# Last six layers of a two-layer transformer kernel: the score band written into PSUM by ScalarE, value products joined per tile, and new orders

## The reference, cut to what matters

```python
def local_attention(q, k, v):          # per batch and head, n = 512 rows, w = 32
    bq = q.reshape(b, h, nw, w, d)
    bk2, bv2 = (look(bk), look(bv))    # window i sees windows i - 1 and i: 64 keys
    mask = (it < jb) | (it > jb + w) | (jb == -1)
    sim = jnp.einsum('bhwie,bhwje->bhwij', bq, bk2) * QK_SCALE
    sim = jnp.where(mask, -jnp.finfo(sim.dtype).max, sim)
    attn = jax.nn.softmax(sim, -1)
    out = jnp.einsum('bhwij,bhwje->bhwie', attn, bv2)

def attn_layer(x, Wqkv, qs, ksc, Wo):  # q and k: l2norm, scale, rotary
    ...
    return out @ Wo

def ffn_layer(x, g, bln, W1, b1, W2, b2):
    xn = (x - mu) / jnp.sqrt(var + 1e-05) * g + bln
    a, gate = jnp.split(xn @ W1 + b1, 2, -1)
    return a * jax.nn.gelu(gate, approximate=False) @ W2 + b2

for i in range(6):
    x = attn_layer(shift_tokens(x), Wqkv[i], q_scale[i], k_scale[i], Wo[i]) + x
    x = ffn_layer(shift_tokens(x), ln_g[i], ln_b[i], W1[i], b1[i], W2[i], b2[i]) + x
```

## Time and profile before

| what | us |
|---|---|
| median of 3 runs (2396.79 to 2399.0) | 2398.37 |
| span of the profiled execution | 2396.9 |
| PE busy in the span | 2203.9 |
| DVE busy | 1780.6 |
| ACT busy | 1719.1 |
| POOL busy | 1230.9 |

### The profile page before, as it was taken

One profiled execution on the slowest core, in us unless ns is written; L12 is line 12 of the kernel. 1 busy time (PEld: TensorE's weight loads), 2 busy tenths in 40 slices (PEclk: granted clock), 3 DMA queues, 4 the chain that ended last, 5 costly groups with the idle time before them and its releaser, 6 DMA issues.

```text
span 2396.9 us, 82108 instructions
## 1 busy us (share of the span) xinstructions
PE 2203.9 (92%) x33332; PEld 1567.5 (65%) x33332; DVE 1780.6 (74%) x3567; ACT 1719.1 (72%) x3982; POOL 1230.9 (51%) x2002
## 2 busy tenths in 40 slices
PE   6799679999976799999999999999999999999996
PEld 3487368888855566666766666666666666666662
DVE  3577377777777788888888888878888888888851
ACT  2255378888854678878888787777778888778771
POOL 0177010000001677776777776767777777767650
PEclk9899789999987899999999999999999999999997
DMA  2000021221102111112111121112111211122110
GB/s 88 10 1 1 22 98 53 80 80 53 71 2 82 30 51 51 51 47 58 51 53 42 54 72 48 45 44 60 50 41 39 75 53 51 36 64 60 40 33 22
DMA packets 40966, 117.73 MB, mean 49 GB/s; under 512 B 7952, under 2 KB 13392, under 8 KB 37776
## 3 DMA queue, kind: packets, MB, share of 16 engines
q1 hardware_dynamic: 40592, 112.49, 15.5%
HBM read 50.48 MB, written 2.23 MB: 22 GB/s over the span
## 4 chain that ended last, share of the span: by engine, by line
PE 49%; ACT 10%; issue 4%; POOL 2%; DVE 2%; DMA 1%; SPq 0%; ACTq 0%; POOLq 0%; DVEq 0%
PE w_psP L1785 12%; PE w_psT L1794 7%; PE w_psF L1729 6%; PE w_psO L1841 6%; PE w_psS L1812 5%; PE w_psF L1751 5%; PE w_psT L1823 3%; ACT w_pb L1893 3%; PE w_psF L1755 2%; PE w_psS L1803 2%; ACT w_sq L1868 1%; ACT L1893 1%; ACT L1917 1%; DMA w_xsf<-H 1%; ACT w_oT L1906 1%
## 5 line engine op out<-in xcount | busy, mean ns | idle before, releaser
L2055 POOL TENSOR_TENSOR w_ab<-w_ab,w_nrm 128x512 f32<-128x512 f32 x384 | 392.9, 1045 | 8.4 <-POOL w_nrm L84 8.4
L1893 ACT ACTIVATE w_pb<-w_psS,w_mx 128x64 f32<-128x64 f32 x1536 | 350.2, 338 | 2.8 <-DVE w_mx L1962 1.9
L2047 POOL TENSOR_TENSOR w_ab<-w_ab,w_bb 128x512 f32<-128x512 f32 x192 | 245.3, 1278 | 172.8 <-DVE w_bb L1946 171.1
L1958 DVE TENSOR_REDUCE w_nrm<-w_sq 128x8 f32<-128x512 f32 x384 | 249.5, 665 | 107.5 <-ACT w_sq L1868 107.3
L1868 ACT ACTIVATE w_sq<-w_psP 128x512 f32<-128x512 f32 x384 | 237.4, 618 | 84.7 <-DVE w_nrm L1958 42.5
L1785 PE MATMUL w_psP<-w_hi,w_xh 128*128 128x512 f32 x576 | 274.6, 477 | 25.0 <-POOL w_xl L2037 8.5
L2071 POOL TENSOR_TENSOR w_pb<-w_pb,w_sm 128x512 f32<-128x512 f32 x192 | 200.3, 1043 | 185.0 <-DVE w_sm L1971 184.5
L1794 PE MATMUL w_psT<-tables_all,w_ab 128*128 128x128 f32 x1536 | 242.0, 280 | 8.7 <-POOL w_ab L2055 4.0
L1197 DVE TENSOR_TENSOR e_glo<-e_hh,e_ghi 128x512 fp32r<-128x512 f32 x256 | 169.3, 685 | 93.0 <-ACT e_ghi L1151 92.9
L1794 PEld LDWEIGHTS w_psT<-tables_all,w_ab 128*128 128x128 f32 x1536 | 174.2, 141 | 87.3 <-ACT w_qT L1881 23.9
L1785 PE MATMUL w_psP<-w_lo,w_xh 128*128 128x512 f32 x576 | 231.1, 401 | 0.0
(11 more groups left out here) (294 smaller groups left out, 5348.5 us busy)
## 6 DMA issues: line engine op xcount, KB each, us to landing
X<-tables_layer SPq DMA_DIRECT2D x48, 384.0 KB, 3.5
X<-w_v SPq DMA_DIRECT2D x48, 384.0 KB, 3.5
e_gb<-gate_rows SPq DMA_DIRECT2D x16, 1024.0 KB, 4.7
e_raw<-in_w_moe SPq DMA_DIRECT2D x32, 256.0 KB, 5.1
w_raw<-in_w_qkv SPq DMA_DIRECT2D x20, 384.0 KB, 4.8
X<-tables_layer SPq DMA_DIRECT2D x48, 128.0 KB, 3.6
w_o<-in_w_o SPq DMA_DIRECT2D x6, 512.0 KB, 4.6
w_xs<-H SPq DMA_DIRECT2D x24, 128.0 KB, 3.3
```

The costliest lines, as they stand in the source:

```text
L1893: last = act.activation(pb[k % 2][:, n, :], psS[:, j, KEYS * q:KEYS * (q + 1)], ACT.Exp, bias=mx[:, n:n + 1])
L1958: dve.tensor_reduce(nrm[k // 2][:, 0, 8 * (i % 8):8 * (i % 8) + 8], sq[:, i % 2, :].rearrange("p (h d) -> p h d", d=DH), AX_X, ALU.add).th ...
L2047: pool.tensor_tensor(a, a, bb[:, i % 2, :], ALU.add).then_inc(s["ad"], 1)
L2055: pool.tensor_tensor(a, a, nrm[k // 2][:, 1, 8 * (i % 8):8 * (i % 8) + 8].unsqueeze(2).to_broadcast([128, 8, DH]), ALU.mult).then_inc(s["n ...
```

## The change

Three things change in `windowed_layers`.

1. The band: PE writes it once, ahead of all rounds. From then on a new ACT unit "Bw k" copies it from `band_bf` into psS behind the exps of block k, and S(k+1) adds its products to that copy. S waits for `s["bw"]` instead of `s["e"]`; Bw waits for `s["e"]` of its own block.
2. Value products: Av k is now one unit per tile, 64 matmuls for its two blocks, even and odd, and Ot one output copy per tile of 1024 columns. pT gets a third buffer. `s["av"]` and `s["ot"]` count tiles instead of blocks.
3. The orders of all five engines are new. The constants `halves` and `guesses`, which nothing here reads, are gone with their memsets.

```diff
--- before.py
+++ after.py
@@ -1537,8 +1537,6 @@
     ab = c.sb("w_ab", [128, 2, 4, 512])
     bb = c.sb("w_bb", [128, 2, 512])
     nrm = [c.sb(f"w_nrm{j}", [128, 4, 64]) for j in range(2)]
-    halves = c.sb("w_halves", [128, 64])
-    guesses = c.sb("w_guesses", [128, 64])
     qT = [c.sb(f"w_qT{j}", [128, PAIRS, 128]) for j in range(2)]
     kT = c.sb("w_kT", [128, PAIRS, WIN + N])
 
@@ -1551,7 +1549,7 @@
     pb = [c.sb(f"w_pb{j}", [128, PAIRS, KEYS]) for j in range(2)]
     mx = c.sb("w_mx", [128, PAIRS])
     sm = [c.sb(f"w_sm{j}", [128, PAIRS]) for j in range(2)]
-    pT = [c.sb(f"w_pT{j}", [128, 4, 128]) for j in range(2)]
+    pT = [c.sb(f"w_pT{j}", [128, 4, 128]) for j in range(3)]
     oT = c.sb("w_oT", [128, PAIRS, N])
     xsf = c.sb("w_xsf", [D, N])
     yn = c.sb("w_yn", [128, TILES, D])
@@ -1565,7 +1563,7 @@
     scl = c.sb("w_scl", [128, 2, 4, DH])
     first = oT[:, 0:6, :].rearrange("p a b -> p (a b)")
 
-    names = ("wa", "wf", "wo", "tab", "scl", "z", "xst", "wd", "wh", "wl", "xh", "xl", "y", "xs", "p", "sq", "ab", "rs", "ad", "nm", "t", "te", "vx", "s", "mx", "e", "r", "pn",
+    names = ("wa", "wf", "wo", "tab", "scl", "z", "xst", "bw", "wd", "wh", "wl", "xh", "xl", "y", "xs", "p", "sq", "ab", "rs", "ad", "nm", "t", "te", "vx", "s", "mx", "e", "r", "pn",
              "pt", "pte", "av", "ot", "f", "xf", "xsf", "yn", "xn", "gg", "hh", "out")
     s = {k: c.sem("w_s_" + k) for k in names}
     s_ve = [c.sem(f"w_s_ve{j}") for j in range(2)]
@@ -1621,30 +1619,30 @@
     ORDER = {
         "pe": """
...
-            V1.1 P2.0 g1-- Av5.0- T0.0 P2.1 a1-- At7.0- Av6.0- T0.1 P2.2 g2-- T0.2 Av7.0-""",
...
+            T2.2- P0.2 At1.0- P0.3 tr-- T2.3- Av0.0- T3.0- S4.0-""",
...
         "sp": """
-            VE2.0-- xd0.0 VE3.0-- wd0.0- t1-- VE0.0- tl- VE1.0- xfd--""",
+            wd0.0------------ tl-------------- xd0.0----------- xfd-------------- t1--------------
+            VE0.0------------- VE1.0------------- VE2.0------------- VE3.0-------------""",
     }
 
@@ -1698,7 +1696,7 @@
                         sp.dma_start(x_back, x_dram).then_inc(s["xst"], 16)
                 elif kind == "VE":
                     wait(sp, s["vx"], r * UV + 2 * k + 2)
-                    wait(sp, s["av"], r * NBLK + 2 * (k - 2) + 1)
+                    wait(sp, s["av"], r * TILES + k - 1)
                     sp.dma_start(v_even[k % 2][WIN:128, :], v[k][0:128 - WIN, :]).then_inc(s_ve[k % 2], 16)
                     if k:
                         sp.dma_start(v_even[k % 2][0:WIN, :], v[k - 1][128 - WIN:128, :]).then_inc(s_ve[k % 2], 16)
@@ -1723,7 +1721,7 @@
                 half = int(f[2])
                 if half == 0:
                     pe.wait_ge(s["wo"], (layer + 1) * 16)
-                    pe.wait_ge(s["ot"], (r + 1) * NBLK)
+                    pe.wait_ge(s["ot"], (r + 1) * TILES)
                     wait(pe, s["out"], r)
                 for pair in range(4 * half, 4 * half + 4):
                     last = pe.matmul(psF[:, :], w_o[:, pair, :], oT[:, pair, :], start=(pair == 0),
@@ -1797,11 +1795,7 @@
                 elif kind == "S":
                     t, e = k // 2, k % 2
                     pe.wait_ge(s["te"], r * UR + 4 * t + 4)
-                    wait(pe, s["e"], r * UE + 2 * k)
-                    for h in range(2):
-                        rows = slice(64 * h, 64 * h + QB)
-                        pe.matmul(psS[:, h, 0:4 * KEYS], c.ident_bf[rows, :], c.band_bf[rows, min(k, 1), :], start=True,
-                                  stop=False, skip_group_check=True)
+                    wait(pe, s["bw"], r * NBLK + k)
                     for g in range(2):
                         for n in range(2):
                             at = QB * (e + 2 * n)
@@ -1824,28 +1818,30 @@
                                             pb[k % 2][:, 2 * q:2 * q + 2, :].rearrange("p a b -> p (a b)"), c.ident[:, :])
                     last.then_inc(s["pt"], 1)
                 elif kind == "Av":
-                    t = k // 2
-                    if k % 2:
-                        pe.wait_ge(s["vx"], r * UV + 2 * t + 2)
-                        vals = v[t]
-                    else:
-                        pe.wait_ge(*ve_done(t, r))
-                        vals = v_even[t % 2]
-                    wait(pe, s["ot"], r * NBLK + k)
-                    pe.wait_ge(s["pte"], r * NBLK + k + 1)
-                    for h in range(2):
-                        for c4 in range(4):
-                            for g in range(2):
-                                for n in range(2):
-                                    rows, head = slice(64 * n, 64 * n + 64), 2 * (4 * g + c4) + h
-                                    last = pe.matmul(psO[64 * g:64 * g + 64, n, QB * (4 * h + c4):QB * (4 * h + c4 + 1)],
-                                                     vals[rows, head * DH:(head + 1) * DH],
-                                                     pT[k % 2][rows, 2 * h + g, QB * c4:QB * c4 + QB], start=True, stop=True,
-                                                     skip_group_check=True)
+                    pe.wait_ge(s["vx"], r * UV + 2 * k + 2)
+                    pe.wait_ge(*ve_done(k, r))
+                    wait(pe, s["ot"], r * TILES + k)
+                    pe.wait_ge(s["pte"], r * NBLK + 2 * k + 2)
+                    for e, vals in enumerate((v_even[k % 2], v[k])):
+                        pt = pT[(r * NBLK + 2 * k + e) % 3]
+                        for h in range(2):
+                            for c4 in range(4):
+                                for g in range(2):
+                                    for n in range(2):
+                                        rows, head = slice(64 * n, 64 * n + 64), 2 * (4 * g + c4) + h
+                                        at = QB * (PAIRS * e + 4 * h + c4)
+                                        last = pe.matmul(psO[64 * g:64 * g + 64, n, at:at + QB],
+                                                         vals[rows, head * DH:(head + 1) * DH],
+                                                         pt[rows, 2 * h + g, QB * c4:QB * c4 + QB], start=True, stop=True,
+                                                         skip_group_check=True)
                     last.then_inc(s["av"], 1)
                 else:
                     mm_tail(pe, k, r, layer)
             pe.wait_ge(s["z"], 2)
+            for h in range(2):
+                rows = slice(64 * h, 64 * h + QB)
+                pe.matmul(psS[:, h, 0:4 * KEYS], c.ident_bf[rows, :], c.band_bf[rows, 0, :], start=True, stop=False,
+                          skip_group_check=True)
             turns(pe, "pe", step)
 
         @block.scalar
@@ -1867,7 +1863,7 @@
                     act.wait_ge(s["p"], r * UP + 6 * k + j + 1)
                     act.activation(sq[:, i % 2, :], psP[j % 2][:, :], ACT.Square).then_inc(s["sq"], 1)
                 elif kind == "Ve":
-                    wait(act, s["av"], (r - 1) * NBLK + 2 * k + 2)
+                    wait(act, s["av"], (r - 1) * TILES + k + 1)
                     wait(act, *ve_done(k, r - 1))
                     if k < TILES - 1:
                         wait(act, *ve_done(k + 1, r - 1))
@@ -1893,18 +1889,21 @@
                         last = act.activation(pb[k % 2][:, n, :], psS[:, j, KEYS * q:KEYS * (q + 1)], ACT.Exp,
                                               bias=mx[:, n:n + 1])
                     last.then_inc(s["e"], 1)
+                elif kind == "Bw":
+                    act.wait_ge(s["e"], r * UE + 2 * k + 2)
+                    act.activation(psS[:, :, 0:4 * KEYS], c.band_bf[:, 0 if k == NBLK - 1 else 1, :].unsqueeze(1).to_broadcast(
+                        [128, 2, 4 * KEYS]), ACT.Copy).then_inc(s["bw"], 1)
                 elif kind == "Pt":
-                    wait(act, s["av"], r * NBLK + k - 1)
+                    wait(act, s["av"], r * TILES + (k - 1) // 2)
                     act.wait_ge(s["pt"], r * NBLK + k + 1)
-                    act.activation(pT[k % 2][:, :, :], psT[:, :].rearrange("p (a b) -> p a b", a=4),
+                    act.activation(pT[(r * NBLK + k) % 3][:, :, :], psT[:, :].rearrange("p (a b) -> p a b", a=4),
                                    ACT.Copy).then_inc(s["pte"], 1)
                 elif kind == "Ot":
                     if k == 0:
                         wait(act, s["f"], (r - 1) * 10 + 1)
-                    act.wait_ge(s["av"], r * NBLK + k + 1)
-                    where = oT[:, :, 128 * (k // 2):128 * (k // 2) + 128].rearrange("p a (n w q) -> p n w a q", n=2, w=2)
-                    act.activation(where[:, :, k % 2, :, :], psO[:, :, 0:QB * PAIRS].rearrange("p n (a q) -> p n a q", q=QB),
-                                   ACT.Copy).then_inc(s["ot"], 1)
+                    act.wait_ge(s["av"], r * TILES + k + 1)
+                    act.activation(oT[:, :, 128 * k:128 * k + 128].rearrange("p a (w q) -> p w a q", w=4),
```

(1 more changed line is left out.)

37 lines of the change are left out of this document (17 added, 20 removed).

## The result

The changed kernel takes 2465.5 us (median of four runs, 2464.3 to 2469.9) against 2398.7 us for the kernel before: ratio 1.028, interval 1.026 to 1.029. The forecast was 2378 us with a range up to 2403, so it missed in sign and in range.

What follows compares the result with a forecast made beforehand. PE was taken as the bound, other engines close; a loop of waits cut the round from 63.9 to 63.2 us. Over 24 rounds -17 us, absorbed disturbance -6, last drain +3: 2377, or 2378 by the median; range 2337 to 2403.

Steps and rivals of the forecast that it cites:

- PE's work, 3.0 us less per round: PE's saving per round: 1.8 us of band matmuls and 1.2 us of value products; alone it would make 63.9 us 60.9.
- 1.2 at most: Value products on PE: joining two blocks saves 0.3 us in each of four tiles, between 0 and 1.2 us a round.
- The disturbance of 1.0 us: Mean round over undisturbed round, from a late transfer or instruction; a quarter absorbed where PE waits anyway, 6 us in all.
- SP's queue: Shifted values queued behind input: at most 2 us late, hidden by PE's wait; five rounds may cost up to 15 us.
- (b): Loop stretch from xf to block 5's row maximum: DVE runs without a gap but for short waits, 17.3 us; PE waits anyway.
- some 2 us of slack: ACT per round: two table loads fewer save 2.6 us, so with the added band copies it gains some 2 us.
- (c): Loop stretch from block 5's row maximum to block 6's scores, through exps and the band copy: 2.6 us.
- (d): Loop stretch from block 6's scores to the next round's first transposition, through exps, a Square and POOL's root: 11.6 us.
- The loop, 63.2 us: Closed path of waits between engines through one round: 63.2 us, range 62.3 to 64.0, so 0.7 of 3.0 us saved arrive.
- Slower: Rival, chance 0.1: a band copy of 1.2 us instead of 0.6 costs 13 us, 2411 us; decides from 0.9 us.
- PE alone: Rival, chance 0.2: only PE's work sets the round, 72 us less, 2327 us; PE over 97% busy.
- The 0.9 us of cheaper entries: Score units on PE: one tiling-mode drain fewer per block, 0.9 us a round; lower case 2306 us, chance 0.02.

Runs made afterwards that it cites:

- e3: Kernel before with only the value products joined, one unit and one output copy per tile, band still on TensorE: 2510.3 us, 1.045.
- e14: e9 with the first half of tile 0's value unit moved between a projection and a transposition, and TensorE laying only bands 6 and 7: 2427.5 us, 1.009.
- e5: Kernel after with SP's transfers of shifted values for tiles 0 and 1 put ahead of the round's two input transfers: 2442.8 us, 1.018.
- e4: Kernel before with only the band change: ScalarE copies the band into the score bank, TensorE's band matmuls removed: 2467.6 us, 1.026.
- e12: Kernel before with ScalarE's band copy at four of eight blocks (0, 3, 4, 7), TensorE's band at the others: 2439.1 us, 1.013.
- e10: e5 with the band of blocks 5, 6 and 7 laid by TensorE again, the other five copied by ScalarE: 2428.8 us, 1.009.
- e7: Kernel after with all bands back on TensorE and no ScalarE band copies, joined values and orders kept: 2468.2 us, 1.028.
- e9: e10 with each joined value unit cut in two, placed so as to delay no transposition, projection or gate unit: 2410.7 us, 1.003.
- e1: Kernel after with each tile's joined value unit cut in two in TensorE's order, another unit between the halves: 2468.1 us, 1.026.
- e6: e5 with each joined value unit cut in two, placed where instruction pages are used up fastest: 2450.4 us, 1.020.
- e13: e9 with only the value units of tiles 1 and 2 cut, and TensorE laying only bands 6 and 7: 2411.9 us, 1.004.

## Why the prediction was wrong, step by step

The forecast of 63.2 us and three quarters of the 1.0 makes a mean round of 63.95 us; it took 67.35. Reckoned as in the table, the forecast held 60.5 us of PE's work and 3.5 of idle time, and the round had 62.9 and 4.4. So of the 3.4 us that were missed, 2.4 are work that didn't go or came back slower (about 1.0 of it is the low clock), and 1.0 is idle time, which moreover stood elsewhere than forecast. The step that failed by size is the 3.0 us of PE's work; the steps that failed by mechanism are the disturbance that was to be absorbed, the transfer that was to be hidden, and the slack on ACT.

**PE's work, 3.0 us less per round.** The band's 1.8 was right (1.71). The value units' "1.2 at most" was taken in full (its own two terms, 0.14 and 0.11 a tile, give 1.0): e3 shows 0.5, and in the kernel after 0.17 is left. And the step counted only what the change removes. By the new order the 24 projection units take 20.85 us instead of 19.58, and they keep that in every kernel with this order. The clock is little of it: outside the stretches of low clock they take 20.75 and 19.57. About half is the one transposition bank: a transposition, one projection, and the next transposition that must wait for ScalarE's copy. In the kernel after, chain of waits at 2033.90 us (start, us, what):

```profile
2033.90 0.45 PE w_psT L1792 x4
...
2034.43 0.61 ACT w_qT L1877
...
2035.09 0.66 PE w_psT L1792 x4
```

1.19 us between two transpositions, between which a projection of 0.70 runs; the wait is not bracketed, since the projection's modelled end covers it. The new order has five such triples where the old one had two, because four value units of 1.1 us that stood between transpositions are gone. I did not look for it, though the earlier trace rows has both widths. In both kernels a projection so placed takes 0.98 to 1.00 us to the next unit, the others 0.80 on the mean before and 0.83 after, so three more triples are 0.6 of the 1.2 us. Another 0.5 stands in one place, the projections P1.3 and V1.0, now side by side behind g0: 1.15 and 0.93 us, before 0.79 and 0.80 apart from each other. What holds them is not shown, and no run took either away: the one that aimed at the triples, e14, made another wait.

**The disturbance of 1.0 us, "absorbed, a quarter".** This is the step that failed in kind. "One instruction came late" was read in the trace of before and left as noise. It was instruction supply: 24 stalls, 0.70 us per round, each on a page boundary. A change that lays 128 value products end to end, with 64 scores before or behind, triples it, to 2.20. The step should have asked what the late rows have in common. It would have found the boundaries; but most of the stalls of before follow late packets, not fast pages, so their size alone did not foretell the rise.

**SP's queue, "at most 2 us late in plain rounds" and hidden.** The place was right, the cover was not. PE did not wait elsewhere in (b), so nothing hid it: 12 of 22 rounds waited, 17.6 us in all, up to 4.11, where at most five late rounds and 15 us were in the range. e5 gives 23 us back. The text named this wait before Av0.0 as what would prove it wrong, if it came in every round; it came in more than half.

**ACT, "some 2 us of slack".** The copy's price was near (0.6 taken, 0.66 measured), the spare loads are there, and yet e4, e12, e10 and e7 all show the copies on the path. Slack over the round was set against work at places: ScalarE gained where the Gelus are and was loaded between tr and the exps of block 6. The prediction saw the copy only as a link in (c) and (d); it is also work in a queue with hardly a gap, where Squares and copies of keys and weights that TensorE needs stand behind it.

**The loop, 63.2 us.** It did not hold the round. PE's wait for POOL before T0.0, expected at 1 to 2 us, is 0.9 us in all rounds together, and before S6 it is 0.17 us per round. The loop was summed over one undisturbed path, and the bound was a mixture that changed from place to place.

**The rivals.** "Slower" was there with 0.1, by a copy of over 0.9 us. The copy took 0.66 and the kernel was slower by five times as much as that case gave. "PE alone" fell by its own row, 93% busy. The 0.9 us of cheaper entries, on which its lower case counted, did not show: without the band ahead of them the scores take more, not less, 6.87 us per round instead of 6.54 in e4, with the low clock nearly as in before, so that the 1.71 us of the band shrink to 1.4.

Taken together: of the 67 us, SP's order gives back 23 (e5), taking three copies off ScalarE 14 (e10), the cuts 18 (e9). These are what edits gave, one upon the other; how much of the 18 is the stalls themselves is not shown (e1, e6 and e13 speak against taking them one to one). The rest, and what the removed matmuls should have brought, is the projections' longer time and what is left of stalls and low clock; these were not separated.

## What to carry to other kernels

Before packing short matmuls more densely, number the engine's instructions and look where its unexplained gaps fall; if they sit at a fixed stride, density can cost time, and a longer unit between two dense ones may be worth more than the joined unit saves, provided that the cut delays no other unit (e9 against e1 and e6). Judge an engine's room at the place where the new work goes, by the chain of waits, not by its busy share: ScalarE was 80% busy and had none. A transfer issued behind another one is only hidden while something else waits. And a term that removes work should also be asked what the units that stay will cost at their new places (here the projections, 1.2 us per round more).

## What the runs showed of the hardware

TensorE's instructions come in 16 KB packets of 256. Where such a page was used up in under 2.5 us, TensorE stood still for over 0.3 us in 234 of 254 cases over all kernels here, and it went on 1.2 to 1.6 us after the packet's end; a page that took longer was followed by a stall when its packet started late. Over 0.3 us this is 51 of 216 page boundaries in the kernel after and 18 of 219 before. By the Trainium skill ("Runtime: NRT & Kernel Launch", Instruction fetch mechanics) such fetches are mostly hidden behind the issue of instructions. The trace does not agree for pairs of weight load and matmul at 12 to 16 ns per pair.

The granted clock was 0.50 in 12 stretches of the 22 rounds of the kernel after, 51 us in all, each behind or during idle time of TensorE of 1.0 to 4.1 us in an otherwise busy stretch. Not every such idle time had one: none followed those of 2.0 us that ended at 1425.9 and 2241.2 us. In a copy into PSUM of 512 columns from bf16, ScalarE takes 0.59 to 0.70 us, as for other copies of this width; one output copy of 1024 columns takes 1.03 us where two of 512 took 1.25.
